# Query products among the splits of Wq's first chunk, and Wk's first product group ahead of the query's bias products

## What is computed

```python
def _L0_xattn_ref(text, features, Wq, bq, Wk, bk):
    Q = jnp.einsum('btx,dx->btd', text, Wq) + bq
    K = jnp.einsum('bpx,dx->bpd', features, Wk) + bk
    scale = 1.0 / jnp.sqrt(jnp.asarray(K.shape[-1], K.dtype))
    scores = jnp.einsum('btd,bpd->btp', Q, K) * scale
    attn = jax.nn.softmax(scores, axis=-1)
    ...
x = x + _L0_xattn_ref(_layernorm(x, axis=-1), ctx_4096, ...)
```

## Time and profile before

| | us |
|---|---|
| median of 3 runs | 922.15 |
| lowest and highest | 921.53 and 922.99 |
| the profiled execution | 922.77 |
| its span in the profile | 920.9 |
| TensorE busy in it | 893.8 |

### The profile page before, as it was taken

One profiled execution on the slowest core, in us unless ns is written; L12 is line 12 of the kernel. 1 busy time (PEld: TensorE's weight loads), 2 busy tenths in 40 slices (PEclk: granted clock), 3 DMA queues, 4 the chain that ended last, 5 costly groups with the idle time before them and its releaser, 6 DMA issues.

```text
span 920.9 us, 19042 instructions
## 1 busy us (share of the span) xinstructions
PE 893.8 (97%) x6866; PEld 817.3 (89%) x6866; DVE 684.5 (74%) x1090; ACT 627.5 (68%) x1093; POOL 488.4 (53%) x334
## 2 busy tenths in 40 slices
PE   8999999999999999999999999999799999999997
PEld 7998888888887799999999999987689999899997
DVE  6446766768446568888888888996988888987754
ACT  5424434565445568888888888886778787887862
POOL 0220000045443897677677777773176667376663
PEclk9999999999999999999999999999999999999999
DMA  8464766778754879565655656555233443224221
GB/s 337 187 255 183 296 238 243 278 259 323 275 193 130 247 225 289 179 216 175 192 174 176 217 175 199 166 203 194 82 137 114 161 148 126 92 93 182 93 92 47
DMA packets 80695, 174.81 MB, mean 190 GB/s; under 512 B 7632, under 2 KB 57584, under 8 KB 78064
## 3 DMA queue, kind: packets, MB, share of 16 engines
q1 hardware_dynamic: 79920, 173.63, 53.9%
q10 hardware_dynamic: 704, 0.23, 0.1%
HBM read 161.51 MB, written 11.53 MB: 188 GB/s over the span
## 4 chain that ended last, share of the span: by engine, by line
PE 77%; DVE 8%; ACT 5%; POOL 3%; DMA 3%; issue 2%; SPq 0%; DVEq 0%; ACTq 0%; POOLq 0%
PE bank L51 19%; PE bank L53 19%; PE bank L52 19%; PE bank L1422 4%; PE bank L1423 3%; PE bank L1393 3%; PE bank L561 2%; PE bank L1818 2%; PE bank L2105 2%; PE bank L1438 2%; POOL W_all L2346 1%; DMA ring<-in_ctx_dram 1%; DMA ring<-in_L_attn_Wq_rope_dram 1%; POOL wl L1017 1%; ACT ring L1902 1%
## 5 line engine op out<-in xcount | busy, mean ns | idle before, releaser
L1017 POOL TENSOR_TENSOR wl<-ring,wh 128x1024 fp32r<-128x1024 f32 x68 | 161.7, 2400 | 0.0
L51 PE MATMUL bank<-act_all,W_all 128*128 128x256 f32 (+1 forms) x512 | 153.9, 301 | 2.3 <-POOL W_all L2346 1.9
L51 PE MATMUL bank<-act_all,wh 128*128 128x256 f32 x512 | 144.5, 282 | 1.4 <-POOL wl L1017 0.8
L52 PE MATMUL bank<-act_all,wh 128*128 128x256 f32 x512 | 144.1, 282 | 0.0
L53 PE MATMUL bank<-act_all,W_all 128*128 128x256 f32 (+1 forms) x512 | 144.0, 281 | 0.0
L53 PE MATMUL bank<-act_all,wl 128*128 128x256 f32 x512 | 143.8, 281 | 0.0
L525 POOL TENSOR_TENSOR xa_WT_l<-ring,xa_WT_h 128x1024 fp32r<-128x1024 f32 x16 | 43.3, 2724 | 175.0 <-ACT xa_WT_h L520 165.1
L2346 POOL TENSOR_TENSOR W_all<-rnd,W_all 128x512 fp32r<-128x512 f32 x72 | 92.2, 1290 | 56.5 <-ACT W_all L2231 51.3
L1630 DVE TENSOR_TENSOR pl<-bank,ph 128x512 f16<-128x512 f32 x128 | 88.1, 688 | 44.4 <-ACT ph L1569 41.6
L1014 POOL CAST wh<-ring 128x1024 fp32r<-128x1024 f32 x68 | 68.8, 1040 | 69.3 <-PE bank L53 63.9
L51 PEld LDWEIGHTS bank<-act_all,W_all 128*128 128x128 f32 x512 | 97.1, 190 | 3.5 <-POOL W_all L2346 2.6
(11 more groups left out here) (279 smaller groups left out, 2571.1 us busy)
## 6 DMA issues: line engine op xcount, KB each, us to landing
ring<-in_ctx_dram SPq DMA_DIRECT2D x16, 2048.0 KB, 8.0
ring<-in_L_attn_Wq_rope_dram SPq DMA_DIRECT2D x32, 1024.0 KB, 6.5
ring<-in_L_ffn_W_dram SPq DMA_DIRECT2D x14, 2048.0 KB, 7.6
panel<-in_L_ffn_W_dram SPq DMA_DIRECT2D x48, 512.0 KB, 4.3
w1p<-in_L_ffn_W_dram SPq DMA_DIRECT2D x16, 512.0 KB, 4.1
ring<-in_L_xattn_Wq_dram SPq DMA_DIRECT2D x2, 2048.0 KB, 11.9
ring<-in_L_xattn_Wk_dram SPq DMA_DIRECT2D x2, 2048.0 KB, 7.8
ring<-in_L_attn_Wo_dram SPq DMA_DIRECT2D x4, 1024.0 KB, 5.0
```

Of the source, the lines that this page charges most:

```text
L51: pe.matmul(out, lh, rh, start=start, stop=False, skip_group_check=True)
L52: pe.matmul(out, lh, rl, start=False, stop=False, skip_group_check=True)
L1017: pool.tensor_tensor(half_of(l, i), half_of(r, i), f32(half_of(h, i)), ALU.subtract).then_inc(w_lo, 1)
```

## The change

Two places of TensorE's queue are written in another order. No other engine's queue changes, and no instruction is added or removed.

First, `main_q` gets a function that it calls behind each product. The first query group now begins straight behind the eight transposes `turn(0, k)`. Behind its product 4 come b1's transpose with its waits, the wait for Wq's second chunk, and `turn(1, 0)`; behind its product 5 comes `turn(1, 1)`. The loop over the second chunk then starts at k = 2, since the first two are done, and its `main_q(pe, 0, 0)` is left out.

Second, the body of the loop over Wk becomes the function `wk_products(i, c)`, and `wk_products(0, 0)` is called ahead of the wait for `ob_lo` at 8 and of the bias products.

```diff
-            def main_q(pe, c, jj):
+            def main_q(pe, c, jj, between=None):
...
                                    (act_h[0][:, k, :], act_l[0][:, k, :]), k == 0, k == KT - 1)
+                    if between is not None:
+                        between(k)
                 last.then_inc(ob_ready, 1)
...
                 for k in range(KT):
                     turn(0, k)
-                pe.wait_ge(in_bias, 64)
-                pe.wait_ge(tb_lo, 8)
-                pe.transpose(bank[7][:, 0:NF], b1rows[:, :], ident[0:NF, 0:NF]).then_inc(b1_ready, 1)
-                landed(pe, 1, USE_WQ)
-                for k in range(KT):
+
+                def first_turns(k):
+
+                    if k == 4:
+                        pe.wait_ge(in_bias, 64)
+                        pe.wait_ge(tb_lo, 8)
+                        pe.transpose(bank[7][:, 0:NF], b1rows[:, :], ident[0:NF, 0:NF]).then_inc(b1_ready, 1)
+                        landed(pe, 1, USE_WQ)
+                    if k in (4, 5):
+                        turn(1, k - 4)
+
+                main_q(pe, 0, 0, first_turns)
+                for k in range(2, KT):
                     if k == 6:
                         pe.wait_ge(a_misc, 1)
                     turn(1, k)
...
                 for jj in range(CH):
                     main_q(pe, 1, jj)
+
+                def wk_products(i, c):
+
+                    v = KT + i
+                    if c == 0:
+                        pe.wait_ge(ob_lo, v - 3)
+                    for j in range(CH):
...
+                    if c == 1:
+                        last.then_inc(ob_ready, 1)
+
+                wk_products(0, 0)
                 pe.wait_ge(ob_lo, KT)
                 pe.wait_ge(tb_lo, YT + 2 * KT)
                 pe.wait_ge(bk_split, 2)
...
+                            if (i, c) != (0, 0):
+                                wk_products(i, c)
```

More of the change, by code:

```diff
@@ L353, in query_tensor @@
                     main_q(pe, 1, jj)
+                def wk_products(i, c):
[3 more added lines that the diff above has]
+                    for j in range(CH):
+                        r = CH * c + j
+                        if j < 2:
+                            pe.wait_ge(wk_dve, 2 * c + j + 1)
+                        else:
+                            pe.wait_ge(wk_pool, 2 * c + j - 1)
+                        last = product(pe, bank[4 + v % 4][:, 0:T],
+                                       (nat_h(c)[:, j, i * P:(i + 1) * P], nat_l(c)[:, j, i * P:(i + 1) * P]),
+                                       (act_h[1][:, r, :], act_l[1][:, r, :]), r == 0, r == KT - 1)
+                    if c == 1:
+                        last.then_inc(ob_ready, 1)
+                wk_products(0, 0)
                 pe.wait_ge(ob_lo, KT)
```

## The result

The kernel after takes 919.04 us (median of 7 runs, 918.32 to 920.04) where the kernel before, run beside it, takes 922.15 (7 runs, 921.53 to 926.07). The ratio is 0.9962 [0.9949, 0.9976]. On the 922.15 us this is a gain of 3.5 us, between 2.2 and 4.7; the two medians by themselves lie 3.1 us apart. The forecast was a gain of 2.64 us. It lies inside that interval, but the measured time, 922.15 x 0.9962 = 918.65 us, lies just under the range's lower end of 918.7.

A forecast was written before the change was run, and what follows sets the result against it. TensorE's queue, busy 97% of the span, was taken to bound the kernel. Gains of 1.4 and 1.24 us summed to 2.64, so 922.15 became 919.5 us, with an 8-in-10 range of 918.7 to 921.0.

The forecast's parts named there:

- What bounds the kernel: Whole span: TensorE's queue, busy 97%, bounds the kernel; time is won only where it stands still or has fewer instructions.
- Place one: 15.4 to 21.9 us: query products among the transposes fill TensorE's waits for VectorE's low halves, gaining 1.4 us.
- The walk: First query group's new queue, priced step by step from 15.39 us: next group starts at 20.41 instead of 21.89, 1.48 us gained.
- The lower bound of 1.15: First query group: 1.48 us less 0.09 for b1's transpose at its whole 0.21 and 0.24 for three switches.
- Place two: 43.7 to 55 us: Wk's first product group, 1.44 us, fills the idle time ahead of the bias products, net 1.24 us.
- The slack of those behind: VectorE's copy and three panel maxima after the bias products: slack before its next split falls from 1.26 to about -0.2 us, harmlessly.
- The load: Third context chunk, issued at 79.76, awaited until 90.21: its chain follows TensorE and moves by the full 2.64 us.
- A: Rival: half arrives, as a side chain, nearest GpSimd's split of Wk's second chunk, moves less than TensorE; 920.8 us, chance 0.08.
- B: Rival: nothing arrives, as the load ending the wait at 90.21 lands when it does now; 922.1 us, chance 0.08.
- C: Rival: slower, as that load and one a step later both take 14.1 us; 925.9 us, chance 0.04.
- D: Rival: waits inside the first query group served slower than 0.14 us, weight switches cost anew; half of 1.4, 920.2 us, chance 0.10.
- the term for the scatter of medians: Whole kernel's time: 0.4 us widening 919.2 to 920.0 into 918.8 to 920.4, from three runs spanning 1.5 us.

The follow-up runs named there:

- The experiment with four groups: Kernel after with all four of Wk's product groups on its first chunk ahead of the query's bias products, not one: 920.76 us, ratio 0.9978 to before.
- place one alone: Kernel before with only the query products moved among the transposes, Wk's first group left behind the bias products: 921.68 us, ratio 0.9991 to before.
- place two alone: Kernel before with only Wk's first product group moved ahead of the bias products: 921.17 us, ratio 0.9986 to before.
- the last version: Kernel after with b1's transpose behind product 3, zero matmuls in the waits at 640 to 685 us, and 8 more at 334 us: 918.87 us, ratio 0.9961 to before.

## Why the prediction was right, and where its range was not

**What bounds the kernel.** Right. TensorE's queue is the kernel, the waits went, and what was taken from its idle time came off the time. No step turned the gain into a new wait. The three measurements of after against before (0.9962, 0.9978, 0.9976) average 0.9972, which is 2.6 us, and the traces give 2.5.

**Place one: 1.4 us forecast, 1.25 measured.** The mechanism was right, the term somewhat too large. The walk said 1.48. Laid over the rows above, moved to the same start: b1's transpose comes 0.08 us later than walked (the products behind a wait step less evenly than by 0.14); it takes 0.17 us and not 0.12 (17.98 to 18.15); and a product behind four transposes takes 0.44 us (18.56 to 19.00), 0.08 more than I gave it, at two places, of which the second four transposes give back 0.06 (19.00 to 19.36). That is 0.08 + 0.05 + 0.16 - 0.06 = 0.23, and 1.48 - 0.23 = 1.25. The lower bound of 1.15 had counted these same switches and b1's price; it was the better walk.

**Place two: 1.24 us forecast, 1.25 measured.** Right in each part: cover, 12 matmuls of 0.12, the bias products 0.19 us later, nothing lost on switches.

**The slack of those behind.** VectorE's split was not late: 0.41 us of slack are left where -0.2 were forecast, because I had let the third maximum queue behind the bias products' copy while it waits for its panel (1.97 us). It cost nothing either way. The experiment with four groups bounds the rest: by the trace, even a delay of three more groups, 4.3 us, brings one wait of 0.5.

**The load.** The question whether the gain survives the third context chunk was answered as forecast: the issue moved from 79.76 to 77.56 with TensorE. Its wait varied between 0.17 and 0.99 us over the profiles, and three list none, so this load adds up to 0.8 us to any single comparison.

**The rivals.** A fell: TensorE has no wait on GpSimd between 10 and 95 us. My argument on GpSimd was no test, though: I compared the pair of operations at 47.45 with the one at 35.94 as if only the later one met a VectorE split. In the trace of after VectorE's splits end at 33.05 + 2.36 = 35.41 and at 44.57 + 2.36 = 46.93, and GpSimd's pairs begin at 34.99 and 46.51, each 0.42 us before such an end. That the pairs took 5.11 and 5.10 us therefore says nothing. The Trainium skill (SBUF — State Buffer, section "SBUF: two separate sides") has the two lock each other out for a whole instruction. The trace of after neither shows this nor rules it out: the first operation of each pair took 2.71 us and the second 2.45 and 2.43. B fell with the load at 77.56. C fell with it: no load of 14 us stood in the way. D is not what happened, but it pointed at the term that was mis-sized.

**The range.** This is the step that failed: of a sum of 2.64 us the traces show 2.50, but the term for the scatter of medians, 0.4 us, was too small, and halved stretches of TensorE's clock weren't in it at all. Three measurements of the same pair of kernels gave 3.5, 2.0 and 2.2 us, up to 1.0 us from the traces. I took the 0.4 from three runs 1.5 us apart, and I took "the granted clock in its top tenth in every slice" for full clock. A slice is 23 us long. A stretch of 3.4 us at half clock lowers its mean by 0.07 and stays a 9. The mean clock of that execution, 0.997, said that something was missing, and short windows of the timeline would have found 3.4 us of it at 687. The mean alone doesn't separate the two: it is 0.997 for the kernel after as well, whose halved stretch lies in its last 5 us, where it mostly waits (0.79 in the last 11 us, row below, against 0.92 before).

```profile
906.00:917.00 11.00, 5.05 (x38) 4.02 (x36) 4.23 (x8) 1.71 (x4) 0.00 (x0) 0.79 0.24 95
```

Each such stretch costs about 1.4 us where TensorE is busy. The profiles have none to three of them, single runs of one kernel spread over nearly 5 us (before: 920.36 to 925.07 in 35 runs), and the median of after moved by 1.4 us between its measurements. The two profiled executions first compared, 920.9 and 916.9, differ by 4.0 us: 2.5 from the change, 1.4 from one halved stretch, and the rest, which nearly cancels, from the start (-0.3), the context's wait (+0.2) and +0.3 between 643 and 685 us (first +0.5 around 645, where TensorE waits longer for VectorE in before, then -0.2).

The halved clock isn't the whole scatter. The third profile of after has no such stretch ahead of its last 10 us either, yet its span is 918.6 us against 916.9. In it TensorE begins with Wq at 12.77 us, 0.53 later, and waits 0.99 us for the context's third chunk, 0.8 more:

```profile
89.14 0.65 PE L579 MATMUL bank<-ident,ring 128*128 128x128 f32 x4 [0.99 <-DMA ring<-in_ctx_dram]
```

The last 0.4 comes in small steps later. What the median of the first measurement owes to the halved clock is not shown. The mean clock over its seven runs of after is 0.9974, over the later ones 0.9968 and 0.9966; at 0.48 us per 0.001 this is 0.3 to 0.4 us, while their medians are 1.3 and 1.4 us higher. For the seven runs of before beside it no clocks are on record. So the profiled pair of 4.0 us is explained, and why that first measurement came out at 3.5 us is open, beyond its being within the scatter of the runs: its interval from 2.2 to 4.7 us holds the 2.5 of the traces.

The two further measurements of after, 0.9978 and 0.9976, give 2.0 and 2.2 us, 920.1 and 919.9 us on the same 922.15, on the other side of the forecast. The forecast of 919.5 was good; the lower end should have been near 918.

**What stays open.** Why an execution has a halved stretch at 338, 650 or 687 us and the next has not. All 12 stretches of the profiles, the last 10 us aside, began while TensorE stood still or within 1.4 us behind a wait of 0.68 to 2.99 us, and they are rarer where the waits are filled: mean clocks of 0.998 and more in 9 of 9 and 8 of 12 runs, against 4 and 2 of 12 beside them. How the chip decides, the runs don't show. A single wait is not enough: the kernel after waited 1.05, 0.28 and 0.69 us ahead of 684.78 and kept 2.4 GHz, the kernel before 0.99, 0.26 and 0.69 and lost it. Open is also whether the change itself makes such stretches rarer: runs with a mean clock of 0.998 and more were 12 of 31 of the kernel after and 19 of 95 of the kernel before, and place one alone (3 of 12) and place two alone (5 of 12) don't settle it.

## What to carry to other kernels

When an engine waits for the fifth of eight pieces, let it consume the first four; and walk the new queue with every switch between kinds of work priced, since these, with b1's transpose, made 0.15 of the 0.23 us by which the walk was too large. Put independent work ahead of a wait, only as much as fills it: one group was worth 1.25 us, four gave 0.5 back. Before a change of under 0.5% is forecast, look for short windows of halved clock in the profile, which a mean over the span or over a slice of it hides, and for waits that end with a load: both tell how far two runs of the same kernel may lie apart. And judge such a change by the start of the same matmul in several traces: here that gave 2.50 to 2.55 us three times, while the ratios gave 2.0 to 3.5.

## What the runs showed of the hardware

- In stretches of 3.4 us, once 6.8, TensorE's granted clock was 0.50 or 0.51 in the middle of a kernel that keeps it busy 97% of the time. They came in some executions only, at three places where it had had idle pieces of 0.3 to 3.0 us, and there matmuls of 128x256 started 0.21 us apart instead of 0.12.
- Zero matmuls in the waits cost nothing measurable (919.87 against 920.23 us) and in the last version came with a mean clock of 0.998 and more in each of 9 runs; within the runs of a kernel, 0.001 of mean clock went with 0.48 us.
- A transpose of 32x32 between products, its wait hidden, cost 0.17 us of TensorE's queue, nearly as much as one and a half matmuls of 128x256 (0.12 us each); when it stood where a half was awaited, nothing.
- The time at which the first 2 MB of Wq land differed by more than a microsecond between executions (first transpose from 11.78 us in the last version to 13.10 with place two alone; 12.24, 12.63 and 12.77 in the three of the kernel after), as much as either place of the change is worth.
